# A graph layer's operand build: degrees first, lookups and attribute sums next, then the count build in strips of 50 destinations with the first aggregation inside it

## The reference

```python
deg = jax.ops.segment_sum(ones, dst, num_segments=n)
dinv = jnp.where(deg > 0, deg ** (-0.5), 0.0)
norm = dinv[src] * dinv[dst]
h = layernorm(x)
for l in range(5):
    edge_fea = concat([edge_attr[:, 3:] @ ew1[l], edge_attr[:, 0:3] @ ew2[l]], axis=-1)
    agg = segment_sum(norm[:, None] * (h[src] + edge_fea), dst, n)
    h = relu(concat([h, agg], axis=1) @ mlp_w[l] + mlp_b[l])
    h = (h - mean(h, 0)) * rsqrt(var(h, 0) + 1e-5) * bn_g[l] + bn_b[l]   # relu but in the last layer
x = x + h
y = sum over the 2 chosen experts e of w_e * (relu(layernorm(x) @ W1[e] + b1[e]) @ W2[e] + b2[e])
return x + y
```

## Time and profile before

| | us |
|---|---|
| median of 3 runs | 1750.41 (1744.72 to 1751.08) |
| profiled execution | 1748.85 |
| its span, first to last instruction | 1746.8 |
| PE busy | 1564.1 (90%) |
| DVE busy | 717.1 (41%) |
| ACT busy | 367.7 (21%) |
| POOL busy | 195.2 (11%) |

### The profile page before, as it was taken

The page is one execution under the profiler, slowest core; times in us unless marked ns, Lnnn a source line. Parts: engine busy times, 40 slices in busy tenths (PEclk is TensorE's granted clock), DMA queues, the critical chain, the costliest instruction groups (busy, mean ns, idle before and its releaser), DMA issues.

```text
span 1746.8 us, 26261 instructions
## 1 busy us (share of the span) xinstructions
PE 1564.1 (90%) x9010; PEld 943.0 (54%) x9011; DVE 717.1 (41%) x1898; ACT 367.7 (21%) x827; POOL 195.2 (11%) x169
## 2 busy tenths in 40 slices
PE   3588887999999989998999989998999963899996
PEld 2476666657667444444545444444545442666664
DVE  6999995874445122012301122012300176333332
ACT  1355554000000140002200140002200141233332
POOL 1011110000000000000000000000000003466664
PEclk9899997999896999998999989999999966999998
DMA  5000003420000000000000000000000463243442
GB/s 105 1 2 1 2 2 106 174 75 1 1 1 14 0 13 1 1 1 14 1 1 1 1 14 1 1 1 13 2 0 18 80 233 110 40 66 61 66 65 41
DMA packets 50421, 57.97 MB, mean 33 GB/s; under 512 B 14415, under 2 KB 41697, under 8 KB 50048
## 3 DMA queue, kind: packets, MB, share of 16 engines
q1 hardware_dynamic: 39552, 41.67, 8.5%
q0 software_dynamic: 10752, 14.69, 5.2%
HBM read 42.36 MB, written 13.99 MB: 32 GB/s over the span
## 4 chain that ended last, share of the span: by engine, by line
PE 73%; DVE 13%; issue 6%; DMA 4%; DVEq 2%; ACT 1%; POOL 1%; SPq 0%; POOLq 0%
PE bank L631 37%; PE bank L712 13%; PE bank L1123 6%; PE bank L1138 5%; DVE cnt L1364 5%; PE bank L1680 4%; DMA slrow<-sl_dram 3%; PE bank L620 2%; PE bank L1129 1%; PE bank L715 1%; PE bank L1608 1%; DVE ohS L1361 1%; PE bank L1115 1%; DVE ohT L1419 1%; PE bank L1089 1%
## 5 line engine op out<-in xcount | busy, mean ns | idle before, releaser
L631 PE MATMUL bank<-at,m 125*128 125x500 fp8e4 (+1 forms) x3500 | 706.6, 359 | 1.3 <-DVE m L599 1.3
L631 PEld LDWEIGHTS bank<-at,m 125*128 125x128 f16 x3500 | 326.6, 101 | 326.2 <-issue 23.3
L640 DVE TENSOR_TENSOR aggT<-bank,dinvB 128x500 f32<-128x500 f32 (+1 forms) x70 | 42.1, 621 | 346.6 <-PE bank L631 335.4
L1608 PE MATMUL bank<-cnt,ohS 128*128 128x313 bf16 x900 | 140.1, 306 | 46.3 <-DVE cnt L1364 43.1
L803 ACT ACTIVATE hT<-bank,prm 128x500 f32<-128x500 f32 (+1 forms) x70 | 40.5, 630 | 593.2 <-PE bank L715 593.2
L1364 DVE TENSOR_SCALAR cnt<-iotaK,keyE,powE 128x626 bf16<-128x626 int16 x450 | 165.4, 438 | 0.0
L1608 PEld LDWEIGHTS bank<-cnt,ohS 128*128 128x128 bf16 x900 | 107.7, 128 | 73.9 <-DVE cnt L1364 54.3
L851 POOL TENSOR_TENSOR idJ<-idJ,wts 125x1400 f32<-125x1400 f32 x2 | 8.0, 4006 | 1222.9 <-DVE idJ L1007 1222.9
L712 PE MATMUL bank<-hT,wcur 128*128 128x500 f32 (+1 forms) x280 | 124.4, 567 | 0.0
L765 DVE BATCH_NORM_STATS2 zst<-hT 128x6 f32<-128x500 f32 (+1 forms) x70 | 40.3, 617 | 198.6 <-ACT hT L803 198.6
L599 DVE SCALAR_TENSOR_TENSOR m<-bank,dinvP,m 125x256 f16<-125x256 f32 x125 | 58.4, 483 | 149.2 <-ACT m L611 148.9
(11 more groups left out here) (294 smaller groups left out, 1298.0 us busy)
## 6 DMA issues: line engine op xcount, KB each, us to landing
slrow<-sl_dram SPq DMA_DIRECT2D x32, 416.0 KB, 4.2
w1s<-in_L_ffn_W SPq DMA_DIRECT2D x1, 4096.0 KB, 15.8
w2s<-in_L_ffn_W SPq DMA_DIRECT2D x1, 4096.0 KB, 20.2
xin<-in_x SPq DMA_DIRECT2D x1, 2800.0 KB
x<-in_x SPq DMA_DIRECT2D x1, 2800.0 KB
out_rows<-x SPq DMA_DIRECT2D x1, 2800.0 KB
xn_dram<-xn SPq DMA_DIRECT2D x1, 2800.0 KB
wraw<-in_L_gnn_mlp_w SPq DMA_DIRECT2D x5, 512.0 KB, 3.8
```

Source lines behind the costliest of these rows:

```text
L631: last = pe.matmul(bank[banks[g]][:, 0:w], m[:, s, k, h * 128:(h + 1) * 128], at[:, s, a:a + w], start=s == 0 and k == 0, stop=s == NT - 1 ...
L1608: last = pe.matmul(bank[GB * (t % 2) + b][:, 0:GC], ohS[r][:, :, j], cnt1[r][:, j, b * GC:(b + 1) * GC], start=r == 0 and j == 0, stop=r = ...
```

## The change

The order becomes: ranges; a histogram of the destinations for the degrees; lookups; `w12`; attribute sums; count build with the first aggregation inside it; linear part.

- The histogram: 16 batches of 26 chunks. DVE compares the destination's tile (25 columns) and its place in the tile (125) with an iota, PE adds up the products of the two in one bank. The degrees no longer come from `at`, and x's normalisation is done at batch 8.
- One-hots are laid out in pairs of chunks: the innermost two elements are two neighbouring chunks, and the chunk table's slice is a pair that is repeated (step 0) over the width.
- Lookups: 26 batches of 16 chunks. A matmul with minus four times the identity on a mask puts all but the wanted tile's column below zero, and one reduction by maximum replaces mask, product and sum. PE does no unit of the aggregation here; x's transposes, ACT's copies and DVE's low halves of `m` go along.
- Windows of W = 50 destinations in place of tiles of 125, 63 of them, and turns of U = 8 chunks in place of 6, a loop over the turns of each. Even and odd windows have a buffer each.
- Attribute sums: `w12` is the stationary operand (12 columns, sliced at a register), the one-hot of 50 columns the moving one; DVE only compares.
- Count build: DVE compares 1024 elements (source's place), compares 2000 (destination and group), and multiplies the first 1024 by the field's power; the multiplication waits for its own comparison. PE accumulates two windows in a bank, opened and closed by a product with zeros. From window 13 on up to 6 units of the aggregation follow each window. ACT's copies to `at` also sum up what the flag checks at the end.
- `at` lies in blocks of 500 destinations. The flag's check and its exchange stand behind the aggregation.
- Two small steps on the experts' slot table.

```diff
-U = 6
+U = 8
+W = 50
+NW = (N + W - 1) // W
-DENSE_L = 3
-DENSE_S = 8
+DENSE_W = 6
...
+        def dense_after(w):
+            done = 0
+            for v in range(w + 1):
+                ready = NT * H * max((v - 3) // (CQ // W), 0)
+                done = min(done + DENSE_W, ready, DENSE)
+            return done
...
+            for b in range(NHB):
...
+                c = b * HB
+                dve.tensor_tensor(ohG[:, b % 2, :, :, :], to_all(iotaT2[:, :, :], HB // 2), by_pairs(dtile[:, c:c + HB], NT), ALU.is_equal)
+                dve.tensor_tensor(ohL[:, b % 2, :, :, :], to_all(iotaL[:, :, :], HB // 2), by_pairs(dplace[:, c:c + HB], P), ALU.is_equal).then_inc(s_hist, 1)
...
+            for w in range(NW):
+                side = w % 2
+                first, mine, before = first_chunk(dve, w), turns(dve, w), turns_before(dve, w)
+                dve.wait_ge(s_iotaD2, w + 1)
+                with dve.Fori(0, mine) as i:
+                    dve.wait_ge(s_freeD[side], before + i + 1)
+                    dve.tensor_tensor(ohD[:, side, :, :, :], to_all(iotaD2[:, side, :, :], U // 2),
+                                      by_pairs(dst3[:, bass.ds(chunk_of(first, i), U)], W), ALU.is_equal).then_inc(s_ohD[side], 1)
...
+            dve.wait_ge(s_s4, NQ)
+            for w in range(NW):
+                first, mine, before = first_chunk(dve, w), turns(dve, w), turns_before(dve, w)
+                dve.wait_ge(s_iotaK, w + 1)
+                with dve.Fori(0, mine) as i:
+                    c = chunk_of(first, i)
+                    dve.wait_ge(s_free[side], before + i + 1)
+                    dve.tensor_tensor(ohS[:, side, :, :, :], to_all(iotaS[:, :, :], U // 2), by_pairs(sl16[:, bass.ds(c, U)], 128), ALU.is_equal).then_inc(s_eq[side], 1)
+                    dve.tensor_tensor(cnt1[:, side, :, :, :], to_all(iotaK[:, side, :, :], U // 2), by_pairs(key16[:, bass.ds(c, U)], GW), ALU.is_equal)
+                    dve.wait_ge(s_eq[side], before + i + 1)
+                    dve.tensor_tensor(ohS[:, side, :, :, :], ohS[:, side, :, :, :], by_pairs(pow16[:, bass.ds(c, U)], 128), ALU.mult).then_inc(s_oh[side], 1)
+                if w == 1:
+                    attribute_sums()
+                if side and w > 1:
+                    nibbles(w // 2 - 1)
...
+                first, mine, before = first_chunk(pe, w), turns(pe, w), turns_before(pe, w)
...
+                with pe.Fori(0, mine) as i:
+                    pe.wait_ge(s_ohD[side], before + i + 1)
+                    c = chunk_of(first, i)
+                    for j in range(U):
+                        last = pe.matmul(out_w, w12[:, bass.ds(c + j, 1), :].rearrange("p a k -> p (a k)"), ohD[:, side, j // 2, :, j % 2], start=False, stop=False)
+                    last.then_inc(s_freeD[side], 1)
```

More of the change, by code:

```diff
@@ L470, in dense_before @@
[L470 to L488, removed]
@@ L490, in tile_turns, with at_block, chunk_of @@
-        def tile_turns(eng, t):
-            first, (middle, before) = first_chunk(eng, t), turns(eng, t)
-            total = eng.value_load(rng[0:1, 3 * NT:3 * NT + 1], min_val=0, max_val=NT * MAX_TURNS)
-            return first, eng.snap(middle + 1), eng.snap(before + 2 * t), eng.snap(total + 2 * NT)
+        S4_BANKS = (2, 3)
+        def at_block(q):
+            a, w = COLS[q]
+            return at[:, NT * a:NT * (a + w)].rearrange("p (s c) -> p s c", c=w)
+        def chunk_of(first, i):
+            return nc.s_assert_within(first + U * i, 0, NCH - 1, skip_runtime_bounds_check_because="a window's turns start before its last chunk")
@@ L521, in gather_pool, with gather_dve @@
                                 pool.sem_inc(s_got, 2)
-        def gather_dve(dve, phase, l):
-            use = phase + (0 if l is None else l)
-            if phase == 0:
+        def gather_dve(dve, l):
+            total = all_turns(dve)
+            if type(l) is int and l == 0:
                 dve.sem_inc(s_gf, U)
@@ L549, in gather_pe @@
-        def gather_pe(pe, phase, l):
-            use = phase + (0 if l is None else l)
-            with pe.Fori(0, NT) as t:
-                first, last_turn, before, total = tile_turns(pe, t)
-                pe.wait_ge(s_ge, NT * use + t + 1)
-                def turn(i, start, stop_):
-                    n = pe.snap(use * total + before + i)
+                dve.wait_ge(s_gt, NT * l + t + 1)
+                tile = bass.ds(t * P, P)
+                dve.tensor_tensor(aggT[:, 0, tile], bank[0][:, 0:P], dinvB[:, tile], ALU.mult)
@@ new lines, in gather_dve, with gather_pe @@
+                dve.tensor_tensor(aggT[:, 1, tile], bank[1][:, 0:P], dinvB[:, tile], ALU.mult).then_inc(s_ge, 1)
+        def gather_pe(pe, l):
+            total = all_turns(pe)
+            with pe.Fori(0, NT) as t:
+                first, mine, before = tile_turns(pe, t)
+                pe.wait_ge(s_ge, NT * l + t + 1)
+                for h in range(H):
+                    pe.matmul(bank[h][:, 0:P], zeros[:, 0:128], nought(P), start=True, stop=False)
+                with pe.Fori(0, mine) as i:
+                    n = pe.snap(l * total + before + i)
@@ new lines, in gather_pe @@
+                        for h in range(H):
+                            for k in range(2):
+                                last = pe.matmul(bank[h][:, 0:P], grow[:, j, k, h * 128:(h + 1) * 128], gsel[:, j, 0:P], start=False, stop=False)
+                        last.then_inc(s_gf, 1)
+                for h in range(H):
+                    last = pe.matmul(bank[h][:, 0:P], zeros[:, 0:128], nought(P), start=False, stop=True)
+                last.then_inc(s_gt, 1)
+            pe.wait_ge(s_ge, NT * l + NT + 1)
@@ L1337, in _ @@
-            dve.wait_ge(s_rng, 1)
-            dve.sem_inc(s_free[1], 1)
-            dve.sem_inc(s_freeD[1], 1)
-            for t in range(NT + 1):
-                if t == 1:
+            step(dve.tensor_copy(row[:, 0:2 * LANES], bank[0][0:1, 0:2 * LANES]))
+            step(dve.tensor_copy(rng[:, 0:2 * LANES], row[:, 0:2 * LANES]))
+            for lanes in (slice(0, NW, 2), slice(1, NW, 2), slice(NW, LANES)):
+                mine = rngf[:, 1, lanes]
+                step(dve.tensor_tensor_scan(rngf[:, 2, lanes], ones[0:1, 0:mine.shape[1]], mine, 0.0, ALU.mult, ALU.add))
@@ L1342, in _ @@
+            dve.wait_ge(s_rng, 1)
+            for side in range(2):
+                dve.sem_inc(s_free[side], 1)
+                dve.sem_inc(s_freeD[side], 1)
+            for b in range(NHB):
+                if b == NHB // 2:
                     dve.wait_ge(s_x, 32)
```

687 lines of the change are left out of this document (340 added, 347 removed).

## The result

The changed kernel takes 1935.74 us (median of 4 runs), the kernel before 1749.79 on the same chip: a ratio of 1.107 (95%: 1.104 to 1.109). The forecast was 1898 in a range of 1820 to 1975. The time is inside the range, but the change was forecast as +149 us and came to +186, so a fifth of the loss needs its own explanation.

What follows compares the result with a forecast made beforehand. Dynamic register loads on the sequencers were to bound the sums and even count windows, DVE the odd ones. The linear part's start moves from 561.8 to 710.5 us (+148.7), the experts add 0.35: 1748.85 + 149 = 1898 us, range 1820 to 1975.

Steps and rivals of the forecast that it cites:

- Bound and sequencer: Attribute sums and count build: register loads, 0.65 us each on PE, no longer hidden; sums 3.5 us a window, 220 us.
- The rival that hides the sequencer's work: Attribute sums and count build: register loads stay hidden, only engine work counts; 161 us less, 1737 us; chance 0.09.
- a wait and the loop's two branches (0.45): Attribute sums, PE's sequencer: 0.45 us a window, beside three loads (1.95) and eight matmuls with a register address (1.0).
- Odd and even places: Count build, DVE: 33 windows with even first chunk take 3.36 us each, 30 odd ones 4.43, from doubled comparisons.
- An odd pair costs nothing: Count build: every turn takes 3.36 us, the stage 238; 34 us less, 1864 us; chance 0.10.
- rows of one pair never run two in a cycle: DVE comparisons: histogram +32 us, mask +5, all 63 count turns 4.43 us (+45); total 1980 us; chance 0.09.
- Histogram, degrees, lookups, parts: Stages ahead of the attribute sums: degrees done at 92.2 us, lookups 77 us (bounds 66 to 88), sums start at 181.
- Count: Count build with aggregation: 272 us, from 403.5 to 675.5, of which the windows on DVE are 244.
- the terms for nibbles (16): Count build, DVE: 0.79 us a pair of windows, in full on 14 odd ones, else mostly in the gap; 16 us.
- ten evictions at 0.6, the attribute steps and seams: 12: Count build: DVE's copies of finished sums out of PSUM, attribute steps and stage seams, 12 us together.
- 3.6 of 8 us: Count build, ACT: five copies of 500 a pair of windows at 0.6 us each and one of 0.6.
- Tail: Behind the start of the first layer's linear part: the experts' two slot steps add 0.35 us.

## Why the prediction was right, point by point

- **Bound and sequencer.** Right, and shown twice: the same engine work without two loads and the loop makes the two stages 141 us shorter, and one load is worth its 0.65 us in each of the 63 windows of the sums. The rival that hides the sequencer's work (1737 us) is out. The term was mis-sized: "a wait and the loop's two branches (0.45)" and an address were 0.85, so 3.78 a window, 15 us.
- **Odd and even places.** Right in both lengths (0.69 and 1.22, 1.19 and 2.23) and in their number, and shown by the copy that starts even. "An odd pair costs nothing" (1864) and "rows of one pair never run two in a cycle" (1980) are both out.
- **Histogram, degrees, lookups, parts.** The sums start at 181.05 where 181 was forecast, partly by luck: the histogram began 1.5 us later than forecast, it and the degrees took 2.7 longer, and the lookups were 72.1 long where 77 included a start of 5. In the four runs whose edits all lie behind that point the sums start at 176.7 to 180.1. The transfer decided the batch, as said: with four buffers it fell from 2.8 to 2.0 us.
- **Count.** Windows right (240 where 244 was forecast); the terms for nibbles (16) and for "ten evictions at 0.6, the attribute steps and seams: 12" failed, 57 measured. They held neither PE's five stops behind ACT (20 us of stage when taken away) nor the nibble steps held up by the iota (9.6); measured each alone, these two add up to the 29 us of excess. I had summed PE and ACT each against DVE's mean (3.6 under 4.2, "3.6 of 8 us") and never followed the order in which ACT's queue serves PE; and I had said of POOL's iota only that it fits in a window's time, not what it lies beside. Its price was wrong as well: 500 elements were put under 1.3 us and take 1.40. Both were to be seen in the order of instructions.
- **Tail.** 0.35 us expected, 1.7 found; not followed up.

The misses, sums +15, count +25, tail +1 and rest -2, are the 39 us between 1898 and the profiled run's 1937.4.

## What to carry to other kernels

Cutting work into more and smaller dynamic pieces moves the bound from engines to sequencers: before it is done, multiply the pieces by their loads, branches and computed addresses, and ask whether a single instruction of the piece is long enough to hide them. Here 63 windows at 1.95 us of loads are 123 us in the sums alone, while PE's busy time over the whole span fell by 33 us (1564.1 to 1531.1) and DVE's rose by 10. And engine totals that fit side by side say nothing about one queue whose next instruction another engine waits for: read the order on ACT and POOL as closely as on the engine that is the bound.

## What the runs showed of the hardware

- A read of one pair of int16 that is repeated along a row costs twice as much from an odd place (2.23 us for 2000 elements against 1.19); a row of six costs a quarter more.
- An int32 `tensor_scalar` on DVE and an int16 iota on POOL hold each other up: in 14 pairs the step lasted 1.60 us instead of 0.41, in 14 others the iota 1.69 instead of 1.40.
- A stop of 4.25 us on PE was followed by a stretch at a granted clock of 0.57, in which 12 products took 1.7 us more.
